# Per-head token scores in one pass over stacked fp32r halves instead of masked blocks in four, with another order of the setup

## The chip, the cores and the metric

The kernel runs on one core of one Trainium2 chip. The metric is the device time of one execution in microseconds (us). TensorE multiplies (PE in the profile, its weight loads PEld), VectorE is DVE, ScalarE is ACT, GpSimd is POOL, and SyncE (SP) issues most of the transfers.

## The reference, cut to what matters

`x` is (16, 128, 320), `ctx` (16, 128, 192), of which the last 4 rows are "extra tokens"; 8 heads of 40.

```python
query = x @ Wq;  keyt = enc @ Wk;  valt = enc @ Wv      # enc: the first 124 rows of ctx
hs = mha(query, keyt, valt)                             # token attention, 128 x 124 per head
ca_q1 = einsum('btc,th->bch', ca, Wq_ca)[:, indices]    # ca: the last 4 rows of ctx
ca_hs1 = mha(ca_q1, x, x)                               # channel attention, 128 x 128 per head
ca_hs2 = mha(ca_hs1 @ Wq, ca @ Wk_ca, ca @ Wv_ca)
out = (hs + ca_hs2) @ Wout + b_out + x
```

`mha` scales by 40 ** -0.5, takes the softmax over keys and weighs the values.

## The kernel before, in words

The 16 batches are worked in 8 pairs: `body` runs as "first", six times as "mid" (a loop of three with two bodies in each) and as "last", between a prologue and an epilogue. In a body, units 0 and 1 are the channel attention of the pair's two batches and units 2 and 3 their token attention. The body also makes the operands of the next pair ("front": QM, QT01, MT, KT2, KT01, XG, MsT, V0, V1) and finishes the output of the pair before ("project"). Each engine has its own order of these steps, written out by hand in its `body`. TensorE's for a mid pair is: scores_turned(0), channel_scores(1), turn_probs3, turn_hidden(0), weigh(0), turn_hidden(1), project(0), KT2, scores_turned(1), token_scores(0), project(1), weigh(1), QM, turn_probs(unit 2), token_scores(1), MT, KT01, XG, QT01, MsT, weigh(2), channel_scores of the next pair, turn_probs(unit 3), V0, V1, weigh(3).

PSUM has eight banks: two for `scores`, two for `turned`, and two rings of two. Ring A (`bank_a`) is drained by ScalarE, ring D (`bank_d`) by VectorE. The lists `of_a` and `of_d` give the order in which pieces take a ring's banks in turn; a piece waits until the one two places ahead is drained (`fill_a`, `fill_d`).

Projections with fp32-like accuracy are made from fp32r halves: a high half (a rounding copy on ScalarE) and a low half (the difference, on VectorE in the prologue and on GpSimd in a body), with eight matmul passes over x (`X_PASSES`) or five over ctx (`C_PASSES`), line 1069. All other products are plain f32 (two instructions per matmul in the profile) or bf16.

Token scores (line 1217) use plain f32. `QM` is query columns 240 to 319 with 32 columns of m behind them (112 rows in all, `KL`), `QT01` the query columns 0 to 239 in two chunks of 120 (three heads each). ScalarE copies both to `qT`, scaled. `KT01` and `KT2` are the keys in the same chunks; VectorE writes them once per head of a chunk, masked by `hmask`, so that other heads' rows are zero: six `k_blocks` (line 797) and two `k_last` (line 804) per pair. One batch's scores are then four matmuls with 372, 124, 248 and 248 columns, against 120 or 112 rows of queries as weights. `MT` turns QM's rows on TensorE, ScalarE copies m out, GpSimd makes `m_stack` in nine steps (lines 434 to 473), and `MsT` turns it; VectorE copies `m_rows`, which the next channel scores need, as they need `pick_ca`.

The SP queue issues, in order: the setup's loads; in each body the two stores, `load_x`, `load_xT`, `load_ctx` and `load_xh`, each behind the semaphore of what they overwrite; and, after the first body, the 16 `vw_stack` copies (line 394), which stack the halves of the extra tokens' values for one fp32r pass. ScalarE's queue issues `wq`, `hmask` and `wqT`.

The prologue on TensorE is: QM, CA0, MT, k2T (`project_ca`, line 1096), MsT, QT01, G0, channel_scores(0), G1, V0, KT2, turn_stack, G2, V1, KT01, XG. `G0` to `G2` are masked products of Wq and the extra tokens' keys; they are made once, by 9, 9 and 6 copies.

## Time and profile before

| | |
|---|---|
| median of 3 runs | 245.86 us (245.26 to 246.77) |
| profiled execution | 247.51 us, span 245.70 us, mean granted clock 0.988 |
| TensorE matmul busy | 224.6 us (91%), 1756 instructions |
| VectorE | 175.7 us (71%) |
| ScalarE | 119.4 us (49%) |
| GpSimd | 52.6 us (21%) |
| DMA | 19.60 MB in 11772 packets |

The span goes from the first to the last instruction; the 1.81 us around it belong to the execution's time. Busy TensorE includes the latency of each matmul, about 0.27 us, which overlaps that of the next; so the pace of a group is read from the starts of the groups around it. A timeline row gives start, length, engine, line, operation, output and inputs, and count; groups may overlap.

### The profile page before, as it was taken

Reading aid. Unit: us, or ns where it says so; the run is one execution under the profiler, and the core shown is the slowest. Engines: PE = TensorE matmul, PEld = TensorE weight load, DVE = VectorE, ACT = ScalarE, POOL = GpSimd, SP = SyncE. Lnnn points to the kernel's source line nnn. Section 1 sums busy time; section 2 is a strip of 40 time slices with the busy share of each in tenths; the row PEclk is TensorE's granted clock in tenths of the full one; section 3 lists DMA queues with packets and bytes.
Section 4 is the critical chain, followed back from the end, with each engine's and each line's share of the span. In section 5 each row is a group of like instructions: output and inputs, shape, how many; then the busy total and the mean of one; then the engine's idle time right before and its main releaser. Section 6 shows DMA issues by size and latency. Waiting matters only on the chain.

```text
span 245.7 us, 5529 instructions
## 1 busy us (share of the span) xinstructions
PE 224.6 (91%) x1756; PEld 208.4 (85%) x1770; DVE 175.7 (71%) x513; ACT 119.4 (49%) x311; POOL 52.6 (21%) x136
## 2 busy tenths in 40 slices
PE   0269999999999999999999999999999999999972
PEld 0269877989989998999899989998999989997971
DVE  2672997678876878587958696769777876877452
ACT  2425745244552664457355545463547552644640
POOL 3140070030322133022403060306030422010010
PEclk9999988999999999999999999999999999999998
DMA  7995023027956200520052003400242002000001
GB/s 220 271 253 182 4 60 108 3 60 145 202 109 191 61 0 29 181 70 1 16 166 91 0 0 118 128 28 0 60 153 60 0 32 75 0 4 27 27 0 56
DMA packets 11772, 19.60 MB, mean 80 GB/s; under 512 B 1437, under 2 KB 7933, under 8 KB 11757
## 3 DMA queue, kind: packets, MB, share of 16 engines
q1 hardware_dynamic: 11343, 18.30, 26.7%
q10 hardware_dynamic: 414, 1.11, 1.6%
q8 instruction: 8, 0.13, 0.2%
q14 instruction: 7, 0.06, 0.1%
HBM read 14.16 MB, written 2.62 MB: 68 GB/s over the span
## 4 chain that ended last, share of the span: by engine, by line
PE 83%; DVE 9%; issue 3%; DMA 2%; ACT 0%; DVEq 0%; SPq 0%; POOL 0%
PE bank_a L1069 15%; PE scores L1217 12%; PE bank_d L1245 11%; PE bank_d L1242 10%; PE bank_d L1300 7%; PE turned L1064 5%; PE bank_d L1069 5%; PE bank_a L1149 4%; PE scores L1189 3%; PE bank_d L1064 3%; PE bank_d L1113 3%; DMA caQ<-in_ca_picked 2%; PE turned L1205 2%; PE scores L1064 1%; PE bank_a L1064 1%
## 5 line engine op out<-in xcount | busy, mean ns | idle before, releaser
L817 DVE TENSOR_REDUCE neg_max<-scores 128x4 f32<-128x512 f32 (+1 forms) x64 | 41.3, 676 | 18.7 <-PE scores L1217 10.7
L622 ACT ACTIVATE probs<-scores,neg_max 128x124 f32<-128x124 f32 x128 | 34.3, 383 | 10.9 <-DVE neg_max L817 10.9
L1069 PE MATMUL bank_a<-xT_r,wq_r 128*120 128x256 f32 (+1 forms) x192 | 28.8, 303 | 10.6 <-DVE xT_r L732 10.6
L1069 PEld LDWEIGHTS bank_a<-xT_r,wq_r 128*120 128x120 f32 (+1 forms) x192 | 25.6, 195 | 10.7 <-issue 10.6
L1242 PEld LDWEIGHTS bank_d<-xg,probsT 128*128 128x128 f32 x256 | 30.1, 192 | 0.8 <-issue 0.5
L1245 PE MATMUL bank_d<-v_sb,probsT 124*128 124x41 f32 x256 | 30.7, 279 | 0.0
L1245 PEld LDWEIGHTS bank_d<-v_sb,probsT 124*128 124x128 f32 x256 | 30.4, 192 | 0.1
L1242 PE MATMUL bank_d<-xg,probsT 128*128 128x33 f32 x256 | 30.1, 272 | 0.4 <-DVE k_blocks L797 0.4
L611 ACT ACTIVATE probsT<-turned 128x512 f32<-128x512 f32 x32 | 17.4, 595 | 23.5 <-PE turned L1205 15.8
L1217 PE MATMUL scores<-k_blocks,qT 120*128 120x372 f32 (+2 forms) x96 | 24.0, 387 | 0.3
L516 ACT ACTIVATE probsT<-turned 124x512 f32<-124x512 f32 x32 | 17.4, 594 | 13.4 <-PE turned L1064 13.0
L1300 PE MATMUL bank_d<-wout_r,hsT_r 128*128 128x320 f32 x128 | 22.5, 315 | 0.9 <-DVE hsT_r L913 0.9
L491 POOL TENSOR_TENSOR hs<-hs,zeros 128x64 f32<-128x64 f32 x16 | 5.1, 319 | 82.4 <-DVE hs L864 82.4
L797 DVE TENSOR_SCALAR k_blocks<-bank_d,hmask 120x248 f32<-120x248 f32 x48 | 19.1, 467 | 4.7 <-PE bank_d L1069 4.7
L1217 PEld LDWEIGHTS scores<-k_blocks,qT 120*128 120x128 f32 x96 | 15.0, 195 | 6.9 <-DVE hsT_r L906 2.3
L1300 PEld LDWEIGHTS bank_d<-wout_r,hsT_r 128*128 128x128 f32 x128 | 19.6, 189 | 1.3 <-DVE hsT_r L913 1.1
L707 DVE COPY ca_less<-scores 32x128 bf16<-32x128 bf16 x64 | 14.1, 220 | 6.4 <-PE scores L1064 5.6
L1069 PE MATMUL bank_d<-ctxT_r,wk_r 128*120 128x248 f32 (+1 forms) x120 | 17.6, 289 | 0.5 <-DVE g_blocks L968 0.5
L516 ACT ACTIVATE qT<-bank_a 112x256 f32<-112x256 f32 (+1 forms) x16 | 8.2, 513 | 19.5 <-PE bank_a L1069 19.5
L1064 PE MATMUL turned<-ident,probs 128*124 128x128 f32 x128 | 16.8, 274 | 0.0
L445 POOL TENSOR_TENSOR xT_r<-xT,xT_r 128x256 fp32r<-128x256 f32 x21 | 14.8, 736 | 8.8 <-DVE ca_stack L836 8.8
L434 POOL TENSOR_TENSOR m_parts<-m,zeros 128x64 bf16<-128x64 f32 x7 | 2.3, 323 | 65.1 <-ACT m L516 65.1
(127 smaller groups left out, 383.4 us busy)
## 6 DMA issues: line engine op xcount, KB each, us to landing
xT<-in_x_cols SPq DMA_DIRECT2D x8, 384.0 KB, 4.2
x_h<-in_x_heads SPq DMA_DIRECT2D x8, 360.0 KB, 3.6
x_sb<-in_x SPq DMA_DIRECT2D x8, 320.0 KB, 3.5
vw_stack<-vw_part SPq DMA_DIRECT2D x16, 160.0 KB, 3.6
out<-out_sb SPq DMA_DIRECT2D x16, 160.0 KB, 1.8
ctxT<-in_ctx_cols SPq DMA_DIRECT2D x8, 256.0 KB, 4.3
wq<-in_Wq ACTq DMA_DIRECT2D x1, 528.0 KB, 5.2
wqT<-in_WqT ACTq DMA_DIRECT2D x1, 506.2 KB, 8.1
```

Source lines behind the costliest of these rows:

```text
L445: gp.tensor_tensor(parts[1][:, c, :], src[:, c, :], parts[0][:, c, :], ALU.subtract).then_inc(done, 1)
L516: return nc.scalar.activation(dst, src, ACT.Copy, scale=scale)
L611: nc.scalar.activation(probsT[:, 4 * half:4 * half + 4, :], turned[half].rearrange("k (h q) -> k h q", h=4), ACT.Exp) \
L622: last = nc.scalar.activation(probs[:, h, 0:keys], scores[half][:, k * keys:(k + 1) * keys], ACT.Exp, bias=neg_max[:, h:h + 1])
L797: ins = v.tensor_scalar(k_blocks[:, c, j], src[0:KC, c * 2 * KEYS:(c + 1) * 2 * KEYS] .rearrange("p (b k) -> p b k", b=2), hmask[:, 0, j, ...
L817: v.tensor_reduce(neg_max[:, 4 * half:4 * half + 4], scores[half][:, 0:4 * keys].rearrange("q (h k) -> q h k", h=4), AX.X, ALU.max, negate ...
L1064: return nc.tensor.transpose(dst, src, (ident if eye is None else eye)[0:rows, 0:rows])
L1069: ins = mm(dst, stationary(w, half, c), moving(w, half, c), start=first and i == 0, stop=last and i == len(steps) - 1)
L1217: last = mm(scores[half][:, col:col + width], qT[0:rows, at.par, c, tok], keys[:, j:j + heads, b, :], start=True, stop=True)
L1242: last = mm(dst[:, h * (HT + 1):(h + 1) * (HT + 1)], probsT[:, h, :], xg[:, b, h, :], start=True, stop=True)
L1245: last = mm(dst[:, h * (D + 1):(h + 1) * (D + 1)], probsT[0:keys, h, :], v_sb[0:keys, at.par, b, h, :], start=True, stop=True)
L1300: ins = mm(dst[:, 0:HID], hsT_r[half][:, b, c, :], wout_r[:, w, :], start=first and i == 0, stop=last and i == len(X_PASSES) - 1)
```

## The change

1. **Token scores.** Queries and keys are split in high and low halves (`q_parts`, `k_parts`: the high one a ScalarE copy, the low one a VectorE difference). For each head, three slots of 40 partitions are stacked by DMA from tile to tile: queries (high, high, low), keys (high, low, high). A batch's scores are eight fp32r matmuls of 120 rows and 124 columns. Nine DMAs for the keys and nine for the queries are added per pair on SP's queue. `k_blocks`, `k_last` and their masks go. QM has 128 rows: 80 of the queries, 16 of zeros, 32 of m; it is copied a second time, as `qm_last`, for MT. `wk` has no padding.
2. **Order of a body.** On TensorE, KT01, QM, QT01, MT stand between weigh(1) and turn_probs(unit 2), and XG and MsT behind token_scores(1). ScalarE and VectorE follow.
3. **Setup.** `Wk_ca` is loaded before `Wk`; TensorE first does 18 bf16 matmuls on zeros of 512 columns; k2T comes before QM and is masked by VectorE; G1 and G2 go to the two `turned` banks, G1 drained by VectorE in three steps; KT2 and KT01 come before V0. The split of Wout moves into the first body.
4. **vw_stack** is laid out by the place in four and then the group, so that its DMAs write whole rows, in two parts around `load_xh` in the first body. Several tiles share memory.

The diff, cut to its core:

```diff
+M_ROW = 96
+QW = QC + M_ROW + HT
+Q_SLOTS, K_SLOTS = (0, 0, 1), (0, 1, 0)
+STACK = 16 * 9
+PLACE = [3 * (h % 3) + h // 3 for h in range(HEADS)]
+WARM = 18
-    return end * ["P3T"] + front * ["QM", "MT", "XG", "QT01", "V0", "V1"]
+    return end * ["P3T"] + front * ["QM", "QT01", "MT", "XG", "V0", "V1"]
-RING_A = Ring(["QM", "MT", "k2T", "QT01", "G0", "V0", "G2", "V1", "XG"],
+RING_A = Ring(["k2T", "QM", "G0", "MT", "QT01", "V0", "V1", "XG"],
-RING_D = Ring(["CA0", "MsT", "G1", "KT2", "KT01"],
+RING_D = Ring(["CA0", "MsT", "KT2", "KT01"],
...
+            def stack_heads(parts, slots, stack_sb, done):
+                for slot, part in enumerate(slots):
+                    for j in range(3):
+                        chunks = NC if j < HEADS - 6 else NC - 1
+                        sp.dma_start(
+                            stack_sb[D * slot:D * slot + D].bitcast(F32)[:, 3 * j:3 * j + chunks, :]
+                                .rearrange("p h n -> p (h n)"),
+                            parts[part][D * j:D * j + D].bitcast(F32)[:, 0:chunks, :]
+                                .rearrange("p c n -> p (c n)")).then_inc(done, 16)
...
             load_ctx(1)
+            sp.wait_ge(q_low, 2)
+            stack_heads(q_parts, Q_SLOTS, q_stack[0], q_stacked)
+            sp.wait_ge(d_drained, RING_D.no("prologue", "KT01")[0] + 1)
+            stack_heads(k_parts, K_SLOTS, k_stack[0], k_stacked)
...
                     load_ctx(pair)
+                if more:
+                    sp.wait_ge(d_drained, k_made)
+                    stack_heads(k_parts, K_SLOTS, k_stack[1 - at.par], k_stacked)
+                    sp.wait_ge(q_low, q_made)
+                    stack_heads(q_parts, Q_SLOTS, q_stack[1 - at.par], q_stacked)
+                if first:
+                    sp.wait_ge(d_drained, RING_D.no(at, "VW3")[0] + 1)
+                    stack_values(0)
+                if more and ahead:
                     sp.wait_ge(a_filled, xg_made)
                     load_xh(pair)
+                if first:
+                    stack_values(1)
...
+            act.wait_ge(a_drained, RING_A.no("prologue", "k2T")[0] + 1)
             front("prologue", "QM")
+            setup("G0")
+            front("prologue", "MT")
...
                 exps(unit(at, 2), KEYS)
                 if more:
+                    high_keys(at, "KT01")
                     front(at, "QM")
+                    front(at, "QT01")
+                    front(at, "MT")
                 turned_copy(unit(at, 2), KEYS)
...
+                v.scalar_tensor_tensor(q_parts[1][0:rows, c, :],
+                                       bank_a[bank][0:rows, 0:(c.stop - c.start) * 2 * S]
+                                       .rearrange("p (c n) -> p c n", n=2 * S), SCALE,
+                                       q_parts[0][0:rows, c, :], ALU.mult, ALU.subtract) \
+                    .then_inc(q_low, 1)
...
+            keys_ca()
+            low_q("prologue", "QM")
+            pick_first(piece("prologue", "CA0"))
             ca_rows_out(piece("prologue", "CA0"), 0).then_inc(d_drained, 1)
             stack_m()
+            front("prologue", "MsT")
+            dve.wait_ge(g_filled, 1)
+            g_heads(turned[0], 1).then_inc(g1_made, 1)
             low_ctx()
+            low_q("prologue", "QT01")
             maxima(0, S)
             split_max(At(0, 0, 0, "first"), 0)
             front("prologue", "KT2")
             place(At(0, 0, 0, "first"), 0)
             front("prologue", "KT01")
...
                     over_heads(at, 1)
+                    front(at, "KT01")
                     softmax3_start(at)
+                    low_q(at, "QM")
+                    low_q(at, "QT01")
                 maxima(unit(at, 3), KEYS)
...
-                for half, runs in enumerate((((0, 0, 3), (1, 0, 1)), ((1, 1, 2), (2, 0, 2)))):
-                    col = 0
-                    for c, j, heads in runs:
-                        width, rows = heads * KEYS, KL if c == 2 else KC
-                        keys = k_last[:, at.par] if c == 2 else k_blocks[:, c]
-                        last = mm(scores[half][:, col:col + width], qT[0:rows, at.par, c, tok],
-                                  keys[:, j:j + heads, b, :],
+                if b == 0:
+                    pe.wait_ge(q_stacked, at.lin(STACK, STACK))
+                    pe.wait_ge(k_stacked, at.lin(STACK, STACK))
+                for half in range(2):
+                    for k in range(4):
+                        last = mm(scores[half][:, k * KEYS:(k + 1) * KEYS],
+                                  q_stack[at.par][:, PLACE[4 * half + k], tok],
+                                  k_stack[at.par][:, PLACE[4 * half + k], keys],
                                   start=True, stop=True)
...
+            pe.wait_ge(cleared, 1)
+            for _ in range(WARM):
+                mm(scores[1][:, :], ca_now[:, 0, 0, :], ca_now[:, 0, :, :].rearrange("p j q -> p (j q)"),
+                   start=True, stop=True)
+            setup("k2T")
             pe.wait_ge(made, 3)
             pe.wait_ge(wq_split, 3)
             front("prologue", "QM")
...
             turn_ca(dst, 0).then_inc(d_filled, 1)
+            setup("G0")
             front("prologue", "MT")
+            setup("G1")
+            setup("G2")
             pe.wait_ge(made, 6)
             front("prologue", "MsT")
             front("prologue", "QT01")
             got_d("prologue", "MsT")
             channel_scores(0, At(0, 0, 0, "first"), 0)
+            pe.wait_ge(w_parts, 2)
+            front("prologue", "KT2")
+            front("prologue", "KT01")
+            turn_stack(At(0, 0, 0, "first"), 0)
+            pe.wait_ge(q_low, 2)
             pe.wait_ge(w_parts, 4)
             front("prologue", "V0")
             front("prologue", "V1")
...
                 weigh(at, 1)
                 if more:
+                    front(at, "KT01")
                     front(at, "QM")
+                    front(at, "QT01")
+                    front(at, "MT")
                 turn_probs(unit(at, 2), KEYS)
                 token_scores(at, 1)
                 if more:
-                    front(at, "MT")
-                if more:
-                    front(at, "KT01")
                     front(at, "XG")
```

XG waits for both `q_low` steps of its pair, and MT for the first, since they read the ring's banks behind ScalarE.

## Rows read from the trace of the kernel before

**Rows 1.** The chain that ended last, shares of the span by engine.
```profile
PE 83%; DVE 9%; issue 3%; DMA 2%; ACT 0%; DVEq 0%; SPq 0%; POOL 0%
```

**Rows 2.** Timeline of TensorE in one steady pair: start us, length us, count last.
```profile
94.90 1.49 PE L1217 MATMUL scores<-k_blocks,qT 120*128 120x372 f32 x6
...
96.46 0.49 PE L1287 MATMUL bank_d<-vw_stack,probs3T 128*128 x1
...
97.97 1.87 PE L1242 MATMUL bank_d<-xg,probsT 128*128 128x33 f32 x16
99.67 1.17 PE L1069 MATMUL bank_a<-xT_r,wq_r 128*112 128x256 f32 x8
100.68 1.03 PE L1064 MATMUL turned<-ident,probs 128*124 128x128 f32 x8
101.55 1.43 PE L1217 MATMUL scores<-k_blocks,qT 120*128 120x372 f32 x6
...
103.36 1.38 PE L1069 MATMUL bank_d<-ctxT_r,wk_r 128*120 128x248 f32 x10
104.58 1.45 PE L1149 MATMUL bank_a<-g_blocks,x_h 120*128 x12
105.84 2.13 PE L1069 MATMUL bank_a<-xT_r,wq_r 128*120 128x256 f32 x16
107.81 0.40 PE L1064 MATMUL bank_d<-ident,m_stack 128*128 128x128 bf16 x4
108.05 1.93 PE L1245 MATMUL bank_d<-v_sb,probsT 124*128 124x41 f32 x16
109.84 0.62 PE L1189 MATMUL scores<-m_rows,ca_now 128*128 128x128 bf16 x8
...
120.66 1.53 PE L1217 MATMUL scores<-k_blocks,qT 120*128 120x372 f32 x6
```

**Rows 3.** TensorE groups by form: shapes, count, busy us, mean ns, idle before.
```profile
L1069 PE MATMUL bank_d<-ctxT_r,wk_r 128*120 128x248 f32 x80 | 11.1, 285 | 0.5 <-DVE g_blocks L968 0.5
```

**Rows 4.** Timeline of VectorE, ScalarE and GpSimd in the same pair.
```profile
94.24 0.56 DVE L906 TENSOR_TENSOR hsT_r<-scores,hsT_r 128x384 fp32r<-128x384 f32 x1
...
104.78 2.39 DVE L797 TENSOR_SCALAR k_blocks<-bank_d,hmask 120x248 f32<-120x248 f32 x6 [0.67 <-PE bank_d L1069]
107.09 0.21 DVE L888 TENSOR_REDUCE sum<-exp 128x16 f32<-128x64 f32 x1
...
109.27 0.42 DVE L707 COPY m_rows<-bank_d 128x512 bf16<-128x512 bf16 x1
...
103.63 0.22 ACT L516 ACTIVATE m<-bank_a 128x64 f32<-128x64 f32 x1 [1.23 <-PE bank_a L1064]
...
108.68 0.66 ACT L516 ACTIVATE qT<-bank_a 120x512 f32<-120x512 f32 x1
...
105.37 0.94 POOL L473 COPY m_stack<-m_parts 128x64 bf16<-128x64 bf16 x5
```

**Rows 5.** Stretches of time (clock, DMA share, GB/s last), vw_stack's issues, their landing.
```profile
36.00:38.00 2.00, 2.00 (x8) 1.25 (x7) 1.93 (x5) 0.82 (x2) 1.26 (x2) 0.50 0.00 0
60.00:66.00 6.00, 5.86 (x54) 5.64 (x55) 5.21 (x16) 4.04 (x9) 2.01 (x4) 1.00 1.00 203
...
55.33 6.98 SPq L394 DMA_DIRECT2D vw_stack<-vw_part  x9
...
vw_stack<-vw_part SPq DMA_DIRECT2D x16, 160.0 KB, 3.6
```

**Rows 6.** Timeline of the prologue and the first token scores, TensorE and ScalarE.
```profile
10.60 2.02 PE L1069 MATMUL bank_a<-xT_r,wq_r 128*112 128x256 f32 x8 [10.60 <-DVE xT_r L732]
...
15.74 2.63 PE L1096 MATMUL bank_a<-caT,wk_ca 96*120 96x64 f32 x12 [1.88 <-issue]
...
22.91 2.76 ACT L516 ACTIVATE g_blocks<-bank_a,hmask 120x192 f32<-120x192 f32 x9 [0.28 <-PE bank_a L1085]
...
37.36 2.04 PE L1217 MATMUL scores<-k_blocks,qT 120*128 120x372 f32 x6
```

More of the change, by code:

```diff
@@ L250, in attention @@
         x_split = sem("x_split")
+        q_low = sem("q_low")
+        k_high = sem("k_high")
+        q_stacked = sem("q_stacked")
+        k_stacked = sem("k_stacked")
         hs_twice = sem("hs_twice")
@@ L676, in body @@
                     high_hidden(at, 1)
+                if more:
+                    high_keys(at, "KT2")
                 exps_turned(unit(at, 1))
@@ L1007, in body @@
                     softmax3_start(at)
-                if more:
-                    front(at, "KT01")
                 if first:
@@ L1370, in body @@
                 if more:
-                    front(at, "MT")
-                if more:
-                    front(at, "KT01")
                     front(at, "XG")
@@ L1377, in body @@
                 if more:
-                    front(at, "QT01")
                     front(at, "MsT")
```

251 lines of the change are left out of this document (146 added, 105 removed).

## The prediction

> **What bounds the kernel now.** I read the chain of waits first, then the PE groups by form, then one steady pair in the timeline. The chain puts 83% of the span on TensorE and 9% on VectorE [rows 1]; that is 204 of 245.7 us, so time taken off TensorE's stream counts unless another engine or a transfer is late in its place. In a steady pair (token_scores(0) at 94.90 to the next one at 120.66, 25.76 us) TensorE has almost no gap [rows 2]. I split that pair in four. The first token_scores takes 96.46 - 94.90 = 1.56; project(1) 1.51; from weigh(1) to the next channel scores 109.84 - 97.97 = 11.87; from there to the next token_scores(0) 10.82. The second token_scores, with its two MT transposes, is 103.36 - 101.55 = 1.81, of which 0.12 are the transposes, so 1.69.
>
> An f32 matmul is issued as two instructions (8 heads in weigh show as x16) and each costs about 2 cycles per column, where these exceed the weight load. An fp32r matmul is one instruction: ten with 248 columns take 104.58 - 103.36 = 1.22, 0.122 each; the f32 instructions of weigh, with 33 or 41 columns, take 1.70 to 1.79 per 16, so 0.106 to 0.112 each, which is what the load of 128 f32 columns allows [rows 2, 3].
>
> **Token scores.** Before, per batch: 992 columns in four f32 matmuls, 1.56 and 1.69. After: eight fp32r matmuls of 124 columns, each with its own load. No row shows fp32r with 124 columns. From below: the load-bound 0.106 of weigh. From above: 248 fp32r columns at 0.122; and, were fp32r with few columns no better than f32, two passes of 124 columns, about 0.21, that is 1.67 per batch and no gain. I take 0.112, nearest to both rows of its kind: 0.90 per batch. Per pair 3.25 - 1.79 = 1.46; over 8 pairs **-11.7**. QM's weights grow from 112 to 128 columns, MT's too, KT2's shrink to 80: QM's eight instructions take 1.01 for 256 columns each, above the 0.106 of a 128-column load, so I put these at nothing (bounds 0.1 per pair either way).
>
> **The middle of the pair.** The new order is weigh(1), KT01, QM, QT01, MT, turn_probs, token_scores(1), XG, MsT, weigh(2), channel scores. From the start of weigh(1), with durations of [rows 2]: KT01 1.70 to 2.92, QM to 3.93, QT01 (1.97) to 5.90, MT to 6.02, turn_probs (0.87) to 6.89, token_scores(1) to 7.79, XG (1.26) to 9.05. Now the helpers. ScalarE copies KT01 high, QM twice and QT01; the last is full at about 6.15 and takes 0.66 [rows 4], to 6.85. Only then comes MT's copy (0.22), to 7.1. From the end of MT's copy to the end of GpSimd's m chain it is 103.85 to 106.31, 2.46 [rows 4], so MsT can start at 9.55: TensorE waits 0.5. Before, m was ready 1.5 us ahead of MsT. VectorE has six k_blocks (2.39, so 0.40 each) and two k_last (0.8 at that price) less, and four splits more: 248 to 512 columns out of PSUM at the price of hsT_r's 0.56 for 384 [rows 4], so 0.4 to 0.75 each, 2.2 together against 3.2: it is relieved by 1 us. But low_q(QT01) ends at 7.6, the second maximum of token_scores(1) at about 9.0, and softmax3_end with pick_ca and m_rows runs 2.6 (107.09 to 109.69) [rows 4]: channel scores at 11.65, just when TensorE, with its wait of 0.5, gets there. So this stretch shrinks from 11.87 to about 11.65 instead of to 11.08. Of token_scores(1)'s 0.79, 0.6 is given back in each of the 6 middle pairs: **+3.6** (bounds 0 and 0.8 per pair). In the first pair the late VW pieces lie between XG and MsT and cover it; the last pair has no front. MT's wait for low_q(QM) costs nothing: VectorE gets there at about 5.5, TensorE at 5.90; without that 0.4 of cover, turn_probs and all behind it slip. XG's wait (7.6 against 7.79) has 0.2 of cover. KT2's high copy on ScalarE (0.38) stands before exps_turned(1), which weigh(1) needs only after project(1): hidden.
>
> **Stacking transfers.** Each pair has 18 new DMAs on SP's queue (9 for keys, 9 for queries; 40 partitions, 2 to 3 KB each), 1.93 MB. Nearest row: vw_stack, also from tile to tile, where all 16 engines were busy (1.00) at 203 GB/s, 3.6 us to land [rows 5]; so 9.5 us of transfer. Issue: vw_stack's nine took 6.98 with the engines full [rows 5], 0.78 each; I take half that for most and keep 14 for all as the upper end. Keys can start at 4.6 (from weigh(1)), queries at 7.6; the last lands at 4.6 + 9.5 + 3 = about 17, or 21 by the dear issue. They are needed at 11.65 + 10.82 = 22.5, so 1.5 to 5 us of cover and I charge nothing. Behind them on the queue stand only load_xh and the next pair's stores, whose data are made later.
>
> The Trainium skill (DMA: Bandwidth & Descriptors, section on why a DMA increments its semaphore by 16 and not by 1) says that a DMA issued from SP uses the largest number of engines up to 16 that divides the partition counts; 40 partitions would give 10. By that rule, at the per-engine rate of vw_stack, 203 x 10/16 = 127 GB/s is an estimate of the stacks' rate, and the last would land at about 23; no row of this trace shows a 40-partition copy. It speaks against the change, and its time is in the first rival.
>
> **Prologue.** Before: QM's operands at 10.60, k2T at 15.74, when wk_ca has landed; TensorE at its lower level by the durations, since QM's eight take 2.02 here and 1.17 in a pair [rows 2, 6] (1.2 GHz, against 2.4). After: wk_ca is issued in wk's place, so k2T at about 10.4 and QM right after; the 18 matmuls on zeros run from 1.5 to 7 or 9, beside loads, and may leave the clock high. But keys_ca, the QM copies, low_q and G0's nine copies (2.76 [rows 6]) stand before MT's copy on ScalarE, which comes at about 17; m_stack about 18.4, MsT as late as before. From there QT01, at the high clock, saves up to 1.4 (16 instructions), and G1 and V0 are off the way. VectorE then decides: by the order of the code and the durations above, g_heads, low_ctx, low_q, maxima and split end near 25 (an estimate), and XG near 28, some 2.5 earlier than before. The first token_scores (37.36 [rows 6]) could come at 34, but the key stack is issued only from about 26.9 and lands between 33.5 and 37. I take **-2.5** (bounds 0 and -5). Cost of the zeros: none while loads run; if they last past 10.4, up to 1.
>
> **Sum** against the profiled execution: 247.51 (span 245.70 and 1.81 around it) - 11.7 + 3.6 - 2.5 = 236.9. It lies 1.65 above the median of the runs, 245.86, so 245.86 - 10.6 = **235.3 us**.
>
> **Rivals.**
> *Stacks land late.* TensorE waits at token_scores(0) for q_stacked. For: 1.93 MB more per pair beside the 1.7 MB of loads and stores now; the rate of a copy over 40 partitions is in no row. Against: 1.5 to 5 us of cover. TensorE waits once the last stack lands later than 22.5 after weigh(1), and the pair is longer than before from 25.76 - 0.90 - 1.51 = 23.35, that is below 1.93 / (23.35 - 4.6 - 2.0) = 115 GB/s. At 105 GB/s it lands at 4.6 + 18.4 + 2.0 = 25.0, 1.65 past that point: 245.9 + 6 x 1.65 - 2.5 = 253. Chance 0.12.
> *Short fp32r matmuls no faster.* No gain in token scores, no new wait at MsT either: 245.86 - 2.5 = 243.4. For: no row with 124 columns. Against: 248 columns at 0.122. Chance 0.12.
> *The middle wait doesn't appear*, since ScalarE or GpSimd are quicker or the wait overlaps another: 245.86 - 11.7 - 3 = 231. Chance 0.18.
> *The clock falls more often.* In 36 to 38 us the granted clock was 0.50 [rows 5], the level of 1.2 GHz, after the first weigh and v2T; no other such stretch lies in the pairs. The short token scores are a kind of work that no row shows. A fall costs about 1.7 (the token scores there took 2.3 instead of 1.6, the rest in proportion). Five more falls eat 8.5: 235.3 + 8.5 = 244. Chance 0.06.
>
> **How the numbers follow.** My forecast has 0.52, with its own range of 231.5 to 240. The range for 8 in 10: from 229.5 (no middle wait and a better prologue) to 246 (short fp32r at no gain; most of the late stacks left out). A measurement tells about 1% here, 243.4 to 248.3 being no change. Faster by over 1%: 0.52 + 0.18 + half of the second rival = 0.76 with rounding; within 1%: 0.12; slower: 0.12.
>
> **What would show it.** Right: token_scores takes 0.9 per batch, eight fp32r matmuls at 0.11; a gap of half a microsecond before MsT with m_stack as releaser; a steady pair of 24.8 to 25.0; stacks landing by 21; MsT in the prologue near 18.4, scores_turned of the first batch near 28. Wrong: 0.2 per short matmul; TensorE waiting for DMA q_stack or k_stack before token_scores(0); falls of the clock in the steady pairs; a gap before MT or XG for q_low.

## The result and the profile after

Kernel after: **248.62 us** median of 4 runs (247.86 to 248.86), beside 245.73 for the kernel before on the same chip; ratio 1.0097, 95% interval 1.0052 to 1.0142. The change costs about 1%, where 235.3 with a range of 229.5 to 246 was forecast. The profiled execution of after took 247.86 us (span 246.1, granted clock 0.965), that of before 247.51. Some executions of most kernels here come out over 1.5% above the shortest of the same kernel; the medians below count them, the ratios leave them out.

I laid the two profiled executions over each other at the token_scores(0) of each pair; this table shows where the time went.

| stretch | before | after | difference | forecast |
|---|---|---|---|---|
| start to the first token_scores | 37.36 | 42.79 | +5.4 | -2.5 |
| first body, to the next token_scores(0) | 31.8 | 36.6 | +4.8 | -1.5 |
| six steady pairs | 154.5 | 147.6 | -6.9 | -5.2 |
| last body, epilogue, last store | 23.84 | 20.83 | -3.0 | -1.5 |
| sum | 247.51 | 247.86 | +0.35 | -10.6 |

So the gain in the pairs is there, and larger than forecast; the setup and the first body give it back. The two profiled executions flatter the change: they differ by 0.35, the medians by 2.9, since the profile of before is a long one of its kernel and that of after the shortest. Of the last row's -3.0, half is no work of the kernel: VectorE's last instruction ends 3.8 us before the end of the span before (241.93 of 245.7) and 2.3 before it after (243.78 of 246.1), so the last store took 1.5 less in that execution.

First the page: shares by engine, the chain by engine, and the new matmul group.

```profile
PE 222.6 (90%) x1774; PEld 205.7 (84%) x1788; DVE 166.4 (68%) x478; ACT 126.8 (52%) x332; POOL 52.4 (21%) x135
...
PE 77%; DVE 7%; SPq 6%; DMA 4%; issue 3%; ACT 2%; DVEq 0%; POOL 0%; ACTq 0%
...
L1329 PE MATMUL scores<-k_stack,q_stack 120*128 120x124 f32 x128 | 18.2, 287 | 5.3 <-DMA k_stack<-k_part 3.9
```

Against [rows 1], TensorE's share of the chain is down from 83% to 77%, and something new stands in it: SP's queue with 6%. That is not a transfer; it is the time SP takes to *issue* the stacks. VectorE is relieved (175.7 to 166.4 us), as forecast.

TensorE's timeline (start, length, engine, line, what, count, the wait before it): prologue, first body, one steady pair.

```profile
10.66 1.59 PE L1205 MATMUL bank_a<-caT,wk_ca 96*120 96x64 f32 x12 [3.38 <-DMA wk_ca<-in_Wk_ca]
12.01 2.06 PE L1177 MATMUL bank_a<-xT_r,wq_r 128*128 128x256 f32 x8
...
21.97 0.48 PE L1172 MATMUL bank_d<-ident,m_stack 128*128 128x128 bf16 x4 [3.90 <-DVE m_stack L1056]
22.21 3.61 PE L1177 MATMUL bank_a<-xT_r,wq_r 128*120 128x256 f32 x16
...
42.79 1.94 PE L1329 MATMUL scores<-k_stack,q_stack 120*128 120x124 f32 x8 [3.88 <-DMA k_stack<-k_part]
44.52 5.89 PE L1222 MATMUL bank_d<-wout_heads,v_blocks 120*128 120x320 f32 x12
50.24 1.87 PE L1354 MATMUL bank_d<-xg,wq 128*128 128x33 f32 x16
...
63.86 1.98 PE L1357 MATMUL bank_d<-v_sb,wq 124*128 124x41 f32 x16 [0.88 <-DVE vw_part L885]
66.38 0.96 PE L1301 MATMUL scores<-m_rows,ca_now 128*128 128x128 bf16 x8 [0.54 <-DVE m_rows L777]
...
104.08 1.08 PE L1329 MATMUL scores<-k_stack,q_stack 120*128 120x124 f32 x8 [0.20 <-DVE hsT_r L1011]
105.00 0.36 PE L1405 MATMUL bank_d<-vw_stack,probs3T 128*128 x1
...
106.37 1.87 PE L1354 MATMUL bank_d<-xg,wq 128*128 128x33 f32 x16
...
114.08 1.50 PE L1260 MATMUL bank_a<-g_blocks,x_h 120*128 x12
115.57 0.40 PE L1172 MATMUL bank_d<-ident,m_stack 128*128 128x128 bf16 x4
...
117.75 0.62 PE L1301 MATMUL scores<-m_rows,ca_now 128*128 128x128 bf16 x8
...
128.76 1.07 PE L1329 MATMUL scores<-k_stack,q_stack 120*128 120x124 f32 x8 [0.29 <-DVE hsT_r L1011]
```

In the steady pair eight short matmuls take 105.00 - 104.08 = 0.92 (forecast 0.90). The pair is 128.76 - 104.08 = 24.68, where [rows 2] had 25.76. From weigh(1) to the next channel scores it is 117.75 - 106.37 = 11.38 against 11.87. The first token scores wait 3.88 us for the stack, and 3.9 more are lost at the first MsT.

The steady MsT shows no wait, since XG's last matmul still counts as busy, but it is late all the same. XG takes 115.57 - 114.08 = 1.49 from start to start where it took 105.84 - 104.58 = 1.26 before [rows 2], and MsT follows GpSimd's last copy into m_stack, which ends at 115.51:

```profile
114.57 0.94 POOL L525 COPY m_stack<-m_parts 128x64 bf16<-128x64 bf16 x5
```

SP's queue, prologue and the same steady pair (start, length, count):

```profile
27.21 6.86 SPq L363 DMA_DIRECT2D q_stack<-q_part  x9
34.11 6.70 SPq L363 DMA_DIRECT2D k_stack<-k_part  x9
...
110.83 6.78 SPq L363 DMA_DIRECT2D k_stack<-k_part  x9
117.72 6.71 SPq L363 DMA_DIRECT2D q_stack<-q_part  x9
```

Nine DMAs take 6.7 to 6.9 us to issue, 0.75 each from one to the next. In the steady pair the last is issued at 124.43. In the prologue TensorE starts 42.79 - 40.81 = 1.98 after the last issue; by that I estimate that it lands near 126.4, 2.3 us before it is needed. In the prologue the same 13.6 us lie on the critical path: the queries' nine stand first, though the keys are what comes last.

Stretches of time (length; busy us and count for PE, PEld, DVE, ACT, POOL; granted clock, DMA share, GB/s):

```profile
11.80:15.30 3.50, 3.50 (x22) 3.41 (x21) 1.52 (x5) 0.65 (x2) 0.00 (x0) 0.51 1.04 282
22.10:25.50 3.40, 3.40 (x19) 3.40 (x18) 2.81 (x5) 0.00 (x0) 1.32 (x2) 0.50 0.02 5
42.50:46.00 3.50, 3.21 (x11) 2.85 (x12) 1.76 (x3) 2.72 (x9) 0.00 (x0) 0.52 0.82 275
46.00:49.40 3.40, 3.40 (x7) 2.05 (x7) 0.98 (x2) 0.77 (x4) 0.00 (x0) 0.50 0.00 0
66.40:69.90 3.50, 3.50 (x25) 3.43 (x26) 2.61 (x8) 1.41 (x3) 0.08 (x1) 0.51 0.46 150
```

The granted clock is at its lower level, 1.2 GHz, behind each long wait of TensorE: after 3.38 us without work before 10.66, after 3.90 before 21.97, after 3.88 before 42.79 (here for 6.9 us, over the VW pieces), and once more behind the two short waits at 63.86 and 66.38. A wait of 1.29 at 29.3 brought none. Before had one such stretch, of about 3.4 us [rows 5], with no long wait ahead of it. So in this execution each long wait is paid a second time; how far the wait is the cause, the experiments tell.

### The profile page after: what moved, and what is told of

Its sections match the earlier page's. It is cut to its first block, busy times and chain, and to the rows that moved or that the text cites. A ratio compares the mean times of both kernels' runs of the same rounds, so it can differ in the third digit from the quotient of the medians.

```text
span 246.1 us, 5792 instructions
## 1 busy us (share of the span) xinstructions
PE 222.6 (90%) x1774; PEld 205.7 (84%) x1788; DVE 166.4 (68%) x478; ACT 126.8 (52%) x332; POOL 52.4 (21%) x135
## 3 DMA queue, kind: packets, MB, share of 16 engines
q1 hardware_dynamic: 16879, 33.79, 42.8%
## 4 chain that ended last, share of the span: by engine, by line
PE 77%; DVE 7%; SPq 6%; DMA 4%; issue 3%; ACT 2%; DVEq 0%; POOL 0%; ACTq 0%
PE bank_a L1177 14%; PE bank_d L1357 10%; PE bank_d L1354 9%; PE bank_d L1418 7%; PE scores L1329 6%; PE turned L1172 6%; SPq L363 5%; PE bank_d L1177 4%; PE bank_a L1260 4%; PE bank_d L1222 4%; DMA wk_ca<-in_Wk_ca 3%; PE scores L1301 3%; PE bank_d L1172 3%; PE turned L1317 2%; PE scores L1172 1%
## 5 line engine op out<-in xcount | busy, mean ns | idle before, releaser
L684 ACT ACTIVATE wqT<-scores,neg_max 128x124 f32<-128x124 f32 x128 | 34.4, 381 | 8.1 <-DVE neg_max L922 8.1
L1357 PE MATMUL bank_d<-v_sb,wq 124*128 124x41 f32 x256 | 30.8, 279 | 0.9 <-DVE vw_part L885 0.9
L1357 PEld LDWEIGHTS bank_d<-v_sb,wq 124*128 124x128 f32 x256 | 30.4, 192 | 1.1 <-DVE vw_part L885 1.1
L1354 PEld LDWEIGHTS bank_d<-xg,wq 128*128 128x128 f32 x256 | 30.2, 192 | 0.8 <-issue 0.5
L1354 PE MATMUL bank_d<-xg,wq 128*128 128x33 f32 x256 | 30.1, 273 | 0.4 <-ACT wq L673 0.4
L569 ACT ACTIVATE wq<-turned 124x512 f32<-124x512 f32 x32 | 17.5, 594 | 17.8 <-PE turned L1172 17.8
L1329 PE MATMUL scores<-k_stack,q_stack 120*128 120x124 f32 x128 | 18.2, 287 | 5.3 <-DMA k_stack<-k_part 3.9
L1329 PEld LDWEIGHTS scores<-k_stack,q_stack 120*128 120x128 f32 x128 | 16.3, 200 | 7.7 <-issue 7.2
L673 ACT ACTIVATE wq<-turned 128x512 f32<-128x512 f32 x32 | 17.3, 592 | 9.2 <-remote 7.6
L1172 PE MATMUL turned<-ident,wqT 128*124 128x128 f32 x128 | 17.8, 283 | 0.3 <-ACT wqT L684 0.3
```

What stands on the lines that cost most here:

```text
L569: return nc.scalar.activation(dst, src, ACT.Copy, scale=scale)
L673: nc.scalar.activation(probsT[:, 4 * half:4 * half + 4, :], turned[half].rearrange("k (h q) -> k h q", h=4), ACT.Exp) \
L684: last = nc.scalar.activation(probs[:, h, 0:keys], scores[half][:, k * keys:(k + 1) * keys], ACT.Exp, bias=neg_max[:, h:h + 1])
L1172: return nc.tensor.transpose(dst, src, (ident if eye is None else eye)[0:rows, 0:rows])
L1329: last = mm(scores[half][:, k * KEYS:(k + 1) * KEYS], q_stack[at.par][:, PLACE[4 * half + k], tok], k_stack[at.par][:, PLACE[4 * half + k] ...
L1354: last = mm(dst[:, h * (HT + 1):(h + 1) * (HT + 1)], probsT[:, h, :], xg[:, b, h, :], start=True, stop=True)
```

## The experiments

All are edits of the kernel after unless another base is named. Times are medians, ratios are to the kernel before on the same chip.

**1. The first pair's stacks left out.** The stacks are zeroed instead of filled, so the first pair's token attention isn't computed; the matmuls stay.

```diff
-            stack_heads(q_parts, Q_SLOTS, q_stack[0], q_stacked)
...
-            stack_heads(k_parts, K_SLOTS, k_stack[0], k_stacked)
...
+            gp.memset(q_stack[0][:].bitcast(F32), 0.0).then_inc(q_stacked, STACK)
+            gp.memset(k_stack[0][:].bitcast(F32), 0.0).then_inc(k_stacked, STACK)
```

> The changed kernel without the prologue's 18 stacking DMAs: the first pair's stacks are zeroed by GpSimd at the start and its token scores wait for no transfer (the first pair's token attention is left out by this; all instructions of TensorE, VectorE and ScalarE stay). Theory A (the queue's issue of 18 DMAs at 0.75 us each is what delays the first token scores, and the idle TensorE then lets its clock fall): the 3.9 us wait before the first token scores goes, the stretch at 0.50 behind it (6.8 us long) goes or shrinks, and the kernel takes 241.5 to 244.5 us instead of 248.6. Rival B (the first body is held by VectorE's late VW pieces and the transfers, so the wait is hidden anyway): at most 1.5 us gained, 247 or more.

Measured: 242.79 us (242.29 to 244.16), ratio 0.9886 (0.9819 to 0.9953); by the ratios 2.1% or 5.2 us less than the kernel after.

```profile
38.50 1.19 PE L1327 MATMUL scores<-k_stack,q_stack 120*128 120x124 f32 x8
40.88 3.47 PE L1220 MATMUL bank_d<-wout_heads,v_blocks 120*128 120x320 f32 x12 [1.19 <-DVE v_blocks L870]
```

No wait before the token scores, and the twelve VW matmuls take 3.47 instead of 5.89: the clock stays up here with the wait gone. The wait and the slow stretch behind it together are the largest cost. (Experiment 7 had no wait here either, and its clock fell all the same; see the last part of this section.)

**2. The wait filled.** The stacks come as late as before, but TensorE multiplies zeros meanwhile.

```diff
+                if b == 0 and at.kind == "first":
...
+                    for _ in range(18):
+                        mm(scores[1][:, :], zeros[:].bitcast(BF16)[:, 0:128],
+                           zeros[:].bitcast(BF16)[:, 0:512], start=True, stop=True)
```

> The changed kernel with 18 bf16 matmuls on zeros (512 columns, into the second bank of scores) on TensorE in the first body, ahead of the wait for the stacks; the wait itself stays. It takes the clock's part alone. Theory A: the matmuls fit into the 3.9 us of waiting, the granted clock stays 1.00 after it, the 12 VW matmuls take 3.3 us instead of 5.7, and the kernel gains 2.5 to 4 us: about 245.5. Rival C (the clock falls there for another reason, such as the VW matmuls themselves): the clock still falls within the next 7 us, gain under 1 us.

Measured: 245.81 us (four runs, 242.82 to 250.31), ratio 0.9896 (0.9812 to 0.998) from the two shorter ones, 2.0% below the kernel after. The profiled execution took 247.47 us, so I read this stretch from it and not its total:

```profile
46.47 3.46 PE L1222 MATMUL bank_d<-wout_heads,v_blocks 120*128 120x320 f32 x12
```

VW is again at 3.46, although the stack comes no sooner (the last K DMA is issued by 42.71, not by 40.81; the zeros run until the token scores at 45.44, about 0.75 longer than the stack would need). The DMAs beside it are the same, so here it was TensorE's idle time that brought the lower clock. From the first token scores to weigh(0) it is 49.76 - 45.44 = 4.32 here and 50.24 - 42.79 = 7.45 in the kernel after: 3.1 us for the clock alone. By the ratios the kernel gains 4.9, with an interval of 2.1 either side on its own ratio, so these do not contradict each other.

**3. MT ahead of G0** on TensorE and ScalarE in the prologue.

```diff
+            front("prologue", "MT")
             setup("G0")
-            front("prologue", "MT")
...
```

> The changed kernel with MT ahead of G0 in the prologue, on TensorE, ScalarE and in the ring, so that m is copied out before G0's nine masked copies. Theory A (MsT comes at 21.97 because MT's copy stands behind G0's copies on ScalarE, 2.6 us, and because m_stack's copies then meet GpSimd's split of Wk): MsT at 18.3 to 19, five m_stack copies in about 0.6 us instead of 1.88, the first token scores still wait for the stacks but 1 to 3 us earlier; kernel 245.5 to 247.5. Rival D (the prologue is held by VectorE's chain g_heads, low_ctx, low_q, maxima whatever MsT does): under 0.7 us gained.

Measured: 245.22 us, but the four runs lie at 241.57, 243.22, 247.22 and 247.42, too far apart for a ratio. The profile (span 239.8):

```profile
18.61 0.38 PE L1172 MATMUL bank_d<-ident,m_stack 128*128 128x128 bf16 x4
18.80 2.14 PE L1177 MATMUL bank_a<-xT_r,wq_r 128*120 128x256 f32 x16
...
38.04 1.35 PE L1329 MATMUL scores<-k_stack,q_stack 120*128 120x124 f32 x8 [3.20 <-DMA k_stack<-k_part]
```

MsT is 3.4 earlier and waits for nothing, QT01 behind it runs at the full clock (2.14 instead of 3.61), and the whole prologue moves up by 4.75. The wait for k_stack stays, since SP's 13.6 us of issue only begin earlier, at 22.48. Whether the median gains is left to experiment 6.

**4. No zeros at the start** (`WARM = 0`).

> The changed kernel without the 18 matmuls on zeros at its start. In its trace they end at 7.3, TensorE waits 3.4 us for wk_ca, k2T runs at the high clock, and QM behind it at half. Theory A: they are worth little, k2T takes 2.6 instead of 1.6 and nothing else changes: 0 to 1.3 us slower. Rival E (they keep the clock for the whole prologue): 3 us slower or more. Rival F (they shift the stretches in which the clock falls later on): faster by 1 us or more.

Measured: 250.82 us (248.51 to 252.14), ratio 1.0193 (1.0098 to 1.0287): 1% or 2.4 us more than the kernel after, between what theories A and E said. The interval overlaps that of the kernel after (1.0052 to 1.0142), so that the zeros pay is likely, and not shown. In the profile k2T takes 2.64 instead of 1.59 and MsT comes at 24.02 instead of 21.97.

```profile
13.40:17.80 4.40, 4.40 (x24) 4.31 (x24) 2.55 (x9) 0.65 (x2) 0.00 (x0) 1.00 1.02 258
```

The granted clock is 1.00 in this stretch, yet QM's eight take 2.05, as long as at 0.50 in the kernel after (2.06). The same holds of the kernel before, whose QM took 2.02 [rows 6] at a granted clock of 1.00. So at the start of a kernel the matmuls' durations show the pace, and the granted clock does not.

**5. The first Q stack issued by GpSimd**, whose queue is free then.

```diff
-            sp.wait_ge(q_low, 2)
-            stack_heads(q_parts, Q_SLOTS, q_stack[0], q_stacked)
...
             low_weight(wv, wv_r, CP - 1, 2)
+            pool.wait_ge(q_low, 2)
+            for slot, part in enumerate(Q_SLOTS):
+                for j in range(3):
...
+                    pool.dma_start(
...
+                        .then_inc(q_first, 16)
```

> The changed kernel with the prologue's nine query DMAs issued by GpSimd instead of SP, so that SP issues the nine key DMAs at once after KT01's low half (31.2). Theory A (issue is serial per queue, 0.75 us each, and it is the issue that makes the last key stack late): the last of SP's is issued at about 38 instead of 40.1, it lands at about 40.5, the wait before the first token scores is 1.5 to 2 us instead of 3.9, and the kernel gains 1.5 to 4 us over 248.6. Rival G (the 16 transfer engines, not the issue, are the limit): the landing moves by under 0.7 us.

Measured: 243.3 us (242.46 to 250.27), ratio 0.9839 (0.9738 to 0.994), 2.6% below the kernel after. The wait falls from 3.88 to 1.48, about as expected, with the first token scores at 38.70. SP's nine keys still take 7.06; GpSimd's nine take 4.72. Only 2.4 of the 4.1 us gained there are the wait's: in this execution the clock also stayed up behind k2T (QM in 1.19), and MsT came 1.45 earlier, at 20.52.

**6. Both, 5 and 3.**

> Both remedies, the query DMAs of the prologue on GpSimd and MT ahead of G0. Theory A: the gains add, first token scores at 35.5 to 37 (42.8 in the changed kernel, 38.0 with MT first alone), 239.5 to 243 us: below both kernels. Rival D/G: no better than MT first alone, about 245.

Measured: 242.45 us (241.98 to 244.16), ratio 0.9825 (0.9741 to 0.9909). GpSimd's, SP's and TensorE's rows:

```profile
24.68 4.72 POOL L542 DMA_DIRECT2D q_stack<-q_part  x9 [0.30 <-POOL wv_r L532]
...
27.06 7.56 SPq L364 DMA_DIRECT2D k_stack<-k_part  x9
...
37.30 1.94 PE L1342 MATMUL scores<-k_stack,q_stack 120*128 120x124 f32 x8 [1.56 <-DMA k_stack<-k_part]
39.03 5.22 PE L1232 MATMUL bank_d<-wout_heads,v_blocks 120*128 120x320 f32 x12
```

This is faster than the kernel before by 1.75% (0.9 to 2.6%) and than the kernel after by 2.7%. By the ratios it can't be told from experiment 5, so that the two gains add is not shown, though the first token scores come 1.4 earlier. They start as early as in the kernel before (37.36 [rows 6]); the rest of the wait, and the slow VW, remain. SP's nine take 7.56 here, beside GpSimd's.

**7. What the issue of one DMA costs.** In the prologue, with the first pair's stacks left as zeros (its token attention isn't computed), six kinds of three DMAs from tile to tile. In order, partitions by f32 per partition: 40 x 768 (as in the diff), 32 x 768, 40 x 256, 120 x 256, 96 x 256, 64 x 128.

```diff
+            for i in range(3):
+                sp.dma_start(qf[40 * i:40 * i + 40, 0:768], zeros[40 * i:40 * i + 40, 0:768]).then_inc(probed, 16)
...
```

> What one tile-to-tile DMA costs SP's queue to issue, by shape. The prologue's 18 stacking DMAs are left out (the first pair's stacks are zeros) and 18 others from a constant tile stand in their place, three each over: 40 partitions x 3072 B, 32 x 3072 B, 40 x 1024 B, 120 x 1024 B, 96 x 1024 B, 64 x 512 B. Theory A (a fixed price of an issue between tiles, whatever the shape): all at 0.6 to 0.75. Rival H (the partition count decides: a count that 16 divides is cheaper): 32, 96 and 64 partitions at 0.35 to 0.45, 40 and 120 at 0.7. Rival I (bytes decide): 3072 B at 0.7, 1024 B and less below 0.5.

Measured (SP's queue, three of each kind, one execution):

```profile
26.77 2.39 SPq L392 DMA_DIRECT2D q_stack<-zeros  x3
29.21 1.89 SPq L394 DMA_DIRECT2D q_stack<-zeros  x3
31.14 2.32 SPq L396 DMA_DIRECT2D q_stack<-zeros  x3
33.50 2.50 SPq L398 DMA_DIRECT2D k_stack<-zeros  x3
36.04 1.84 SPq L400 DMA_DIRECT2D k_stack<-zeros  x3
37.92 1.88 SPq L402 DMA_DIRECT2D k_stack<-zeros  x3
```

40 partitions cost 0.80 and 0.77 each (3 KB or 1 KB per partition), 120 partitions 0.83; 32, 96 and 64 partitions 0.63, 0.61, 0.63. So the bytes do not matter (a third of them saves 0.03), nor does the number of partitions as such: 96 are as cheap as 32. The counts that 16 divides are cheaper by 0.15 to 0.2: rival H has the direction right and the size wrong. The loads of ctx beside them take SP 0.35. The price is per DMA; fewer DMAs, another queue, or counts that 16 divides would lower it.

The token scores here wait for no transfer, as in experiment 1, but VW is slow:

```profile
41.06 6.02 PE L1238 MATMUL bank_d<-wout_heads,v_blocks 120*128 120x320 f32 x12
```

**8. Token scores in plain f32** over the same stacks.

```diff
-                                  q_stack[at.par][:, PLACE[4 * half + k], tok],
-                                  k_stack[at.par][:, PLACE[4 * half + k], keys],
+                                  q_stack[at.par][:, PLACE[4 * half + k], tok].bitcast(F32),
+                                  k_stack[at.par][:, PLACE[4 * half + k], keys].bitcast(F32),
```

> The changed kernel with its eight token-score matmuls per batch read as plain f32, so two instructions each, with everything else kept. It sizes the term of the stacked halves. If an instruction with 124 columns costs what its weight load allows (0.11), a batch takes 1.8 us instead of 0.9, and a steady pair 25.8 to 26.5 instead of 24.6; kernel about 258 to 263. If the shorter scores were mostly given back in waits behind them, the steady pair grows by under 0.8.

Measured: 260.42 us (259.72 to 265.88), ratio 1.052 (1.0416 to 1.0624).

```profile
106.30 2.02 PE L1329 MATMUL scores<-k_stack,q_stack 120*128 120x124 f32 x16 [0.21 <-DVE hsT_r L1011]
...
132.68 2.02 PE L1329 MATMUL scores<-k_stack,q_stack 120*128 120x124 f32 x16 [0.29 <-DVE hsT_r L1011]
```

Sixteen instructions now, 2.02 instead of 1.08, and the pair takes 132.68 - 106.30 = 26.38 instead of 24.6: +1.8. From start to start a batch's scores take 1.78 instead of 0.92, so twice 0.86 or 1.7. The longer token scores are passed on to the pair in full.

This run shows a second thing. Its first body has the same two short waits as the kernel after, 0.88 for vw_part and 0.54 for m_rows, but the clock does not fall behind them:

```profile
67.70:71.20 3.50, 3.48 (x36) 3.39 (x36) 2.87 (x9) 2.15 (x4) 0.17 (x1) 1.00 0.62 173
```

(The kernel after had 0.51 in the 3.5 us from its channel scores, 66.40 to 69.90.) The second fall is thus missing where the token scores are longer, in one execution. It doesn't hang on the fall before it: in experiment 1 the clock stayed up until 59.8 and then fell behind waits of 0.89 and 0.45. Whether it takes the short token scores, the waits, or both, is not shown.

**9. GpSimd's split of Wk behind m_stack.**

```diff
+            pool.wait_ge(m_step, 9)
             low_weight(wk, wk_r, CP - 1, 1)
```

> GpSimd's split of Wk and Wv waits until all nine steps of m_stack are done; nothing else differs from the kernel after. Theory A: in the prologue VectorE's bf16 copies into m_stack are slowed by GpSimd's tensor operations beside them (five took 1.88 us, against 0.53 in the kernel before, where GpSimd was idle). Then the five take 0.5 to 0.6 here, MsT starts near 20.6 instead of 21.97, but KT2 waits for wk_r. The time stays within 1 us of the kernel after. Rival B: the copies are slow for a reason of their own (their addresses, the lower place of the tiles that now share memory): they take 1.9 again and MsT is not earlier.

Measured: 245.91 us (243.57 to 248.48), ratio 0.9954 (0.9909 to 0.9999). VectorE's five copies in the kernel after, GpSimd's work beside them there, and then the same copies here:

```profile
19.82 1.88 DVE L777 COPY m_stack<-m_parts 128x64 bf16<-128x64 bf16 x5
```
```profile
19.78 0.86 POOL L530 TENSOR_TENSOR wk_r<-raw_kv,wk_r 128x320 fp32r<-128x320 f32 x1 [16.71 <-ACT wk_r L569]
```
```profile
21.28 0.52 DVE L778 COPY m_stack<-m_parts 128x64 bf16<-128x64 bf16 x5
```

Theory A holds for the copies: 0.52 with GpSimd quiet, 1.88 beside it. In the kernel after two of the five, at 19.82 and 20.76, take 0.85 each, beside GpSimd's instructions of 0.86 at 19.78 and 20.72; the others take 0.17. MsT is at 22.08 all the same, since in this execution ScalarE's copy of m came 1.5 later (20.25 instead of 18.78); with that taken off it would be the expected 20.6. By the ratios the kernel gains 1.4%, more than expected. Behind the shorter wait at MsT (2.55 instead of 3.90) the clock did not fall, and QT01 took 2.15 instead of 3.61; the rest I can't place.

**10. The first K stack on two queues as well**: from kernel 6, GpSimd issues four of the nine behind its Q stack.

> As the kernel with the prologue's Q stack issued by GpSimd and MT ahead of G0 (242.45 us, token scores waiting 1.56 for k_stack), and of the nine DMAs of the first K stack four are now issued by GpSimd behind its nine of the Q stack; SP keeps five. Theory A (the issue of the DMAs, one after the other on one queue, is what the first token scores wait for): SP's five end near 31, GpSimd's near 32, the stacks land before 35, the wait of 1.56 is gone, first token scores near 35.7; 1.5 us less than that kernel, about 240.9. Rival B (the transfers themselves or something on TensorE are the limit): the wait stays at 1 or more, or what is gained comes back in the first body; 242.4.

Measured: 243.6 us, ratio 0.9853 (0.9766 to 0.9941), no better than kernel 6. In the profiled execution (247.14 us, the longest of its four) SP's five took 3.98 and GpSimd's four 2.02, but the token scores still waited 1.04. GpSimd's four landed 3.9 and 4.7 us after their issue, the load of x_h beside them 6.3. This fits rival B, that the transfers count once the issue is spread, as far as that execution can tell.

**11. The same with 33 matmuls on zeros** (`WARM = 33`).

> As the kernel with the split K stack, with 33 instead of 18 matmuls on zeros at the start, so that they fill TensorE's idle stretch from 7.3 to 10.7 us. Theory A (an idle stretch of TensorE of over 3 us is what brings the lower clock of 11.8 to 15.3 behind it): granted clock 1.00 there, QM's eight in 1.2 instead of 2.06, another 0.8 to 1.5 us gained at MsT and after, about 239.5. Rival B (the fall has another cause, or VectorE and the transfers set the prologue): the clock still falls after 12, or MsT comes earlier without any gain at the first token scores; within 0.5 of the kernel with the split alone.

Measured: 242.26 us (241.49 to 245.05), ratio 0.9801 (0.9719 to 0.9882). The profiled execution was the longest of its five:

```profile
11.31 1.47 PE L1230 MATMUL bank_a<-caT,wk_ca 96*120 96x64 f32 x12 [0.35 <-DMA wk_ca<-in_Wk_ca]
12.59 1.19 PE L1202 MATMUL bank_a<-xT_r,wq_r 128*128 128x256 f32 x8
...
18.33 0.38 PE L1197 MATMUL bank_d<-ident,m_stack 128*128 128x128 bf16 x4
...
39.65 1.94 PE L1357 MATMUL scores<-k_stack,q_stack 120*128 120x124 f32 x8 [4.57 <-DMA k_stack<-k_part]
```

With no idle stretch ahead of k2T the clock stays up there, as theory A said: QM's eight take 1.19. But k2T starts 0.6 later, behind the last zeros, and MsT is at 18.33 where kernel 6 had 18.52, so rival B is right about the gain. And here the wait for k_stack is 4.57, with all of it issued by 31.3: x_h, issued at 30.93, took 9.2 us to land and GpSimd's four 5.4 and 6.2.

**12. The same, with the next x_h loaded after both stacks.**

```diff
+            sp.wait_ge(k_stacked, 80)
+            sp.wait_ge(q_first, 16 * 13)
             load_xh(1)
```

> As the kernel with the split K stack and 33 matmuls on zeros (242.26 us), where GpSimd's part of the first K stack landed 5.4 to 6.2 us after its issue and TensorE waited 4.57 for it, beside a load of x_h of 360 KB that took 9.2 to land; here that load of the next pair's x_h is issued only when both first stacks have landed. Theory A (with the issue spread over two queues, the stacks now share the DMA engines with that load, and this delays them): GpSimd's four land about 3 us after their issue, the first token scores start between 35 and 36.5 with a wait under 1.5, and the kernel takes 240 to 241.5. Rival B (the landing is slow for another reason, the two queues' own packets beside each other): the wait stays at 3 or more and the time at 242 or above.

Measured: **241.69 us** (239.95 to 243.11, 6 runs), ratio **0.981** (0.9757 to 0.9863).

```profile
36.25 1.08 PE L1359 MATMUL scores<-k_stack,q_stack 120*128 120x124 f32 x8 [1.74 <-DMA k_stack<-k_part]
37.17 5.14 PE L1249 MATMUL bank_d<-wout_heads,v_blocks 120*128 120x320 f32 x12
```

The first token scores start at 36.25, 6.5 earlier than in the kernel after, and the profile is the shortest of all (span 238.1). The wait is 1.74, a little over what was expected, and GpSimd's four still take 4.2 and 4.4 to land, with x_h away: theory A would explain most of the 4.57, and rival B the rest, but both rest on one execution each, and that with 4.57 was the longest of its kernel. The time, 241.69, lies between what the two said. By the medians 11 and 12 can't be told apart; both are 1.9 to 2.0% below the kernel before, and by the ratios 2.8 to 2.9% below the kernel after.

**What the clock did in all of them.** At MsT in the prologue the relation is plain. Seven profiles have a wait of 3.6 to 3.9 there (after, 1, 2, 4, 5, 7, 8), and in all seven the granted clock goes to 0.50 between 0.5 before its end and 1.4 behind it, for some 3 us; six have none or, in 9, one of 2.55 (3, 6, 9, 10, 11, 12), and in none does it fall there (in 10 it had been down until then). For the fall at the first VW pieces a wait can bring it (experiments 1 and 2), but is not needed. It came behind waits of 3.88, 3.71 and 3.20 (after, 9, 3), and of 1.48 and 1.74 (5, 12). In 2, 4, 6, 7, 8, 10 and 11 the clock was down before the stack's wait, or what stood in its place, from 32 to 39 us on, though no wait in the 8 us ahead was over 1.1. Kernel 6 shows it, its wait for the stack starting only at 35.74:

```profile
32.50:42.50 10.00, 8.44 (x29) 6.07 (x29) 5.12 (x11) 3.50 (x11) 4.94 (x6) 0.50 0.52 165
```

So the lower clock at VW can't be put down to the wait alone.

## Why the prediction was wrong, by its steps

**Token scores, -11.7: right.** 0.92 per batch against 0.90 taken; experiment 8 shows that longer token scores lengthen the pair by as much. The rival of short fp32r matmuls without gain falls.

**The middle of the pair, +3.6: wrong, on the good side.** The chain was the right one, MT's copy, GpSimd's nine steps, MsT, but it holds MsT up by 0.2 us and not by 0.5: MsT comes 9.20 after weigh(1), where I had 9.55. From weigh(1) to channel scores it is 11.38, between my 11.65 and the 11.08 of no wait. The waits that TensorE shows in the steady pair, 0.20 and 0.29 for hsT_r ahead of token_scores(0), I did not have. Half of the third rival came true, with 0.3 of its 0.6 per pair, and it is the reason for -6.9 instead of -5.2.

**Stacking transfers, 0: right in the steady pairs, with the wrong price per issue.** I took half of vw_stack's 0.78 per issue as likely and kept 14 us for all as the upper end. 13.5 is what it is, and experiment 7 shows why: 0.6 to 0.8 is the price of a DMA from tile to tile on SP's queue, not a sign of full DMA engines. The steady pairs have room for that (2.3 us of cover), so nothing is lost there. The Trainium skill (DMA: Bandwidth & Descriptors, section on why a DMA increments its semaphore by 16 and not by 1) would have given 10 engines and an estimated 127 GB/s; from 114 to 124 us, with almost nothing but stacks moving, the trace shows 142 GB/s at a share of 0.39, set by the issue. So the rate that the rule was to warn of didn't appear, and the number of engines stays open.

**Prologue, -2.5 with bounds 0 and -5: this is the step that failed.** It came out at +5.4, 7.9 off, in two halves. TensorE reached the first token scores at 42.79 - 3.88 = 38.91, not at 34.9; then it waited 3.88 more.
- The late front, 4.3 of it: I had MsT at 18.4, and it was 21.97. ScalarE's m copy came at 18.78 instead of 17, behind G0's nine copies and behind a stretch at the lower clock from 11.8 that I did not expect after the zeros; then the m_stack copies took 1.88 instead of 0.53. Experiment 3 shows the order's part, 9 the copies', and 5, where the clock happened to stay up, has MsT 1.45 earlier. The wait at MsT then slowed QT01 by 1.5.
- The late stack, 3.6 of it: I wrote that it would be issued from 26.9 and land between 33.5 and 37. As far as I can redo it, that is nine DMAs at half and at whole price and 3 us to land. It left out the nine DMAs of the Q stack that stand ahead on the same queue. With what was measured, 27.2 + 2 x 6.8 + 2 = 42.8, which is what TensorE saw. By my own front the Q stack could start at about 22.9, as VectorE's low half of QT01 ends 4.0 before that of KT01 (27.18 and 31.20 in the kernel after); with my own upper end of 14 us for 18 issues this gives 22.9 + 14 + 2 = 38.9, and with the measured 13.6 it gives 38.5. So the terms were on my table; I used them for the steady pair and not here. Experiment 3 is that case: MsT at 18.61, Q stack from 22.48, first token scores at 38.04. The stack alone would have turned the gain of 2.5 into a loss of about 1.

**The first body, -1.5, not worked out apart: +4.8.** I priced the bodies as if all were alike. The VW pieces at the lower clock cost 5.72 from start to start instead of 3.24 before, 2.5; the waits for vw_part and m_rows cost 1.4; the next fall of the clock behind them stretches the way from channel scores through V0 and V1 (66.38 to 71.32, 4.94, against 117.75 to 120.56, 2.81) by 2.1. That is 6.0 of the 6.3 missed. Experiments 1 and 2 show the price of the first part, and that it can be had back by taking the wait away or filling it; experiment 7, with no wait and VW in 6.02, shows that the wait is not its only cause. The second fall stands at the same place in the profiles of all changed kernels here but that of experiment 8, where the waits are the same and the token scores are f32. Its cause stays open: no run has tried the waits alone.

**The rivals.** "Stacks land late" was the right mechanism at the wrong place: I placed it in the steady pairs at 115 GB/s, and it happened once, in the prologue, by issue. "The clock falls more often" was the other part, with 0.06: not in the steady pairs, as I had it, but in the setup and the first body. I saw the fall after the first weigh in the trace of before and did not ask what TensorE had done ahead of it. Two small rivals came true together, which is why the time lies outside a range that was built from one at a time.

## What to carry to other kernels

Price a DMA by its issue as well as by its bytes, and count all that stand ahead of it on its queue, above all where there is no previous iteration to hide it. A pair in the steady state and the first pair are two sums: what is free in the loop can lie wholly on the critical path of the setup. And an idle stretch of TensorE can be paid again in the granted clock behind it, as at MsT here, so removing a wait, or filling it, can give back more than its length. Look at the clock ahead of the wait too: where it was down already, as in kernel 6, that wait did not bring it down.

## What the runs showed of the hardware that I had not expected

- A DMA from tile to tile costs SP's queue 0.71 to 0.83 us where the partition count is 40 or 120, about 0.6 where it is 32, 64 or 96, whatever the bytes between 0.5 and 3 KB per partition; the loads from HBM cost 0.35 to 0.68 in the prologue of the kernel after. GpSimd issues the same DMAs in 0.52 each.
- After 3.4 to 3.9 us without work for TensorE the granted clock was 0.50 for 3.4 to 6.9 us, and twelve matmuls of 320 columns took 5.89 instead of 3.46. With zeros multiplied in the gap the twelve took 3.46. They came out slow (5.14) behind waits of 1.48 and 1.74 too, and once without a wait (6.02). The length of the wait alone does not tell: waits of 2.87 ahead of k2T (5) and 2.55 ahead of MsT (9) brought no fall, one of 2.30 ahead of k2T (9) did.
- The clock also fell behind two waits of 0.88 and 0.54 where the token scores were short fp32r matmuls, and not in the one execution where they were f32.
- Without work ahead of them the first matmuls ran at the lower pace with a granted clock of 1.00: QM's eight in 2.02 in the kernel before, and in 2.05 without the zeros.
- Five small bf16 copies of VectorE took 1.88 beside GpSimd's subtraction and 0.52 without it; two of them took 0.85 instead of 0.17, as long as GpSimd's instruction beside them (0.86). The Trainium skill (SBUF — State Buffer, section "Who interferes with whom") says that copies in a two-port mode and GpSimd lock each other out for a whole instruction; the trace agrees.
- The load of 360 KB for the second pair, which landed in 3.6 to 3.9 us in the kernels after, 5, 6 and 12, took 6.3 (10) and 9.2 (11) beside stacks issued on two queues at once, in one execution each.
